# Loading the next group's keys and queries in ten parts of 128 KB, spread over the scores of the current group

## What is computed

```python
x = x + 0.5 * ffn(layernorm(x))
x = x + attention(layernorm(x))       # 16 heads of 16, softmax(q k^T / 4) v, then wo and bo
x = x + 0.5 * ffn(layernorm(x))       # same weights

def ffn(x):                            # k0, k1, k2 are boolean: +1 or -1
    h = relu(s0 * (concat([x, -x]) @ sign(k0))) * 2     # 512 -> 1024
    h = relu(s1 * (h @ sign(k1))) * 2                   # 1024 -> 1024
    return s2 * (h @ sign(k2))                          # 1024 -> 256
```

## Time and profile before

| what | us |
|---|---|
| median of 3 runs (range) | 1506.63 (1505.17 to 1507.43) |
| the profiled execution, its own time | 1504.11 |
| its span, first to last instruction | 1500.2 |
| PE busy / PEld / ACT / DVE / POOL | 1476.9 / 763.4 / 1152.1 / 594.8 / 60.0 |
| mean granted TensorE clock | 0.999 |

### The profile page before, as it was taken

One profiled execution on the slowest core, in us unless ns is written; L12 is line 12 of the kernel. 1 busy time (PEld: TensorE's weight loads), 2 busy tenths in 40 slices (PEclk: granted clock), 3 DMA queues, 4 the chain that ended last, 5 costly groups with the idle time before them and its releaser, 6 DMA issues.

```text
span 1500.2 us, 69702 instructions
## 1 busy us (share of the span) xinstructions
PE 1476.9 (98%) x32431; PEld 763.4 (51%) x32431; DVE 594.8 (40%) x1330; ACT 1152.1 (77%) x1240; POOL 60.0 (4%) x65
## 2 busy tenths in 40 slices
PE   9999999999999999999999999999999999999999
PEld 4555455444455445545454454455455565445454
DVE  7546755612431253334332332342342342333462
ACT  3221221899898999999999998999999999999721
POOL 2010011001000100010100000000000000000000
PEclk9999999999999999999999999999999999999999
DMA  4121324313221331233223123113112212212010
GB/s 139 44 85 43 85 71 113 87 42 98 70 56 47 104 102 58 60 101 100 84 56 89 52 51 103 43 49 106 43 42 70 85 43 70 85 58 54 25 42 17
DMA packets 110285, 103.91 MB, mean 69 GB/s; under 512 B 55846, under 2 KB 95526, under 8 KB 109990
## 3 DMA queue, kind: packets, MB, share of 16 engines
q1 hardware_dynamic: 109158, 98.60, 23.5%
q10 hardware_dynamic: 832, 0.79, 0.2%
HBM read 61.87 MB, written 25.43 MB: 58 GB/s over the span
## 4 chain that ended last, share of the span: by engine, by line
PE 97%; issue 1%; DVE 1%; DMA 1%; ACT 0%; SPq 0%; ACTq 0%
PE psum L870 31%; PE psum L911 30%; PE psum L891 15%; PE psum L764 12%; PE psum L776 3%; PE psum L752 3%; PE psum L783 2%; PE psum L796 1%; DMA den_t<-den_rows 0%; DMA x_sb<-in_x 0%; PE psum L789 0%; ACT prob L966 0%; DVE den_t L1130 0%; DVE xn L996 0%; SPq L1268 0%
## 5 line engine op out<-in xcount | busy, mean ns | idle before, releaser
L966 ACT ACTIVATE prob<-psum 128x1024 f32<-128x1024 f32 x1024 | 1033.7, 1025 | 72.8 <-PE psum L891 33.6
L911 PE MATMUL psum<-prob,v_sb 64*17 64x512 f32 x8192 | 559.6, 589 | 2.5 <-issue 1.8
L891 PE MATMUL psum<-q_st,k_st 64*32 64x512 f16 (+1 forms) x7736 | 500.6, 376 | 2.6 <-issue 2.5
L939 ACT ACTIVATE h_hi<-psum 128x512 f16<-128x512 f32 x183 | 108.3, 597 | 219.0 <-PE psum L764 167.5
L891 PEld LDWEIGHTS psum<-q_st,k_st 64*32 64x32 f16 (+1 forms) x7736 | 162.0, 92 | 196.4 <-ACT prob L966 68.2
L911 PEld LDWEIGHTS psum<-prob,v_sb 64*17 64x17 f32 x8192 | 157.6, 93 | 150.7 <-issue 72.7
L1004 DVE TENSOR_SCALAR h_hi<-psum 128x512 f16<-128x512 f32 x73 | 50.5, 692 | 385.9 <-PE psum L870 385.9
L1006 DVE SCALAR_TENSOR_TENSOR h_lo<-psum,h_hi 128x512 f16<-128x512 f32 x256 | 168.2, 687 | 82.9 <-ACT h_hi L939 80.4
L870 PE MATMUL psum<-h_lo,w 64*32 64x512 f16 (+1 forms) x4688 | 167.7, 376 | 6.1 <-issue 6.1
L870 PE MATMUL psum<-h_hi,w 64*32 64x512 f16 (+1 forms) x4688 | 164.5, 376 | 1.6 <-issue 1.3
L870 PEld LDWEIGHTS psum<-h_hi,w 64*32 64x32 f16 (+1 forms) x4688 | 83.8, 93 | 65.0 <-issue 10.3
(11 more groups left out here) (110 smaller groups left out, 884.1 us busy)
## 6 DMA issues: line engine op xcount, KB each, us to landing
k_st<-k_halves SPq DMA_DIRECT2D x64, 512.0 KB, 4.5
q_halves<-piece SPq DMA_DIRECT2D x32, 256.0 KB, 2.5
q_st<-q_halves SPq DMA_DIRECT2D x64, 128.0 KB, 4.9
x_rows<-x_sb SPq DMA_DIRECT2D x16, 256.0 KB, 2.2
k_halves<-piece SPq DMA_DIRECT2D x16, 256.0 KB, 2.8
att_rows<-o_sb SPq DMA_DIRECT2D x128, 32.0 KB
x_sb<-x_rows SPq DMA_DIRECT2D x8, 512.0 KB, 4.3
att_t<-att_rows SPq DMA_DIRECT2D x16, 256.0 KB
```

The costliest lines, as they stand in the source:

```text
L891: mm = pe.matmul(psum[c, SCORES[(h + r) % len(SCORES)], :], k_st[rows, slot, t * P:(t + 1) * P][:, c], q_st[rows, slot, :], start=True, st ...
L911: mm = pe.matmul(psum[32 * j:32 * j + va, O_BANKS[r], :], v_sb[rows, b * key_tiles + t, GROUP * g4 + j, :], prob[rows, h % PROBS, :], star ...
L939: act.activation(hi, psum[:, bank, :], ACT.Relu).then_inc(act_done, 1)
L966: act.activation(prob[:, to:to + 2, :], psum[:, bank:bank + 2, :], ACT.Exp, scale=score_scale / QK_SCALE ** 2).then_inc(exp_sem, 1)
```

## The change

The four transfers of a group become ten. A `k_st` slot is loaded in four parts of 32 partitions (128 KB each), a `q_st` slot stays one transfer of 128 KB. The parts of group g + 1 are no longer issued together at the first score of group g, but at its turns 0, 2, 5, 7, 10, 12, 15, 17, 20 and 22 (`KEY_TURNS`): `lay_score` lays a step "keys" ahead of those scores, and `sp_keys` waits by `qk_sem` until PE has finished all scores that stand ahead. The count that PE waits for at a group's first score rises from 16 x 4 to 16 x 10. The bytes are the same. PE, ACT, DVE and POOL have the same instructions in the same order; only SP's list is different, by six more transfers in each of the 32 groups.

```diff
--- before.py
+++ after.py
@@ -276,6 +276,9 @@
 
 
 
+    KEY_PARTS = 4
+    GROUP_SCORES = group_steps * STEP_BANKS // 2
+    KEY_TURNS = [5 * k // 2 for k in range(2 * (KEY_PARTS + 1))]
     scores_left = [numbers.held[bank] for bank in SCORES]
 
     def lay_score(no, narrow=False):
@@ -283,6 +286,8 @@
         n, pair = divmod(no, STEP_BANKS // 2)
         if pair == 0:
             work.append(Step("att", n))
+        if no % GROUP_SCORES in KEY_TURNS and no // GROUP_SCORES + 1 < groups:
+            work.append(Step("keys", no // GROUP_SCORES + 1, KEY_TURNS.index(no % GROUP_SCORES)))
         work.append(Step("score", n, pair, narrow=narrow))
 
     def lay_values(tile):
@@ -547,7 +552,7 @@
         FACTOR0, SCALARS = 4, 10
         WEIGHTS_IN = 16 * 10
         LN_STEPS = 2 * tpb + 13
-        STAGE = 16 * 2 * 2
+        STAGE = 16 * 2 * (KEY_PARTS + 1)
         O_MOVE = 16 * 2 * GROUP
 
         x_tiles = x.rearrange("b s d -> (b s) d").rearrange("(t p) d -> p t d", p=P)
@@ -1186,15 +1191,13 @@
         def sp_steps(steps):
             for s in steps:
                 u, m = s.u, s.m
-                if s.kind == "att":
-                    if s.u % group_steps == 0:
-                        g = s.u // group_steps
-                        if g + 1 < groups:
-                            sp_stage(g + 1)
+                if s.kind == "keys":
+                    sp_keys(u, m)
                 elif s.kind == "o":
                     sp_o(u)
                 elif s.kind == "stage":
-                    sp_stage(u)
+                    for part in range(2 * (KEY_PARTS + 1)):
+                        sp_keys(0, part)
                 elif s.kind == "load":
                     sp_load(u)
                 elif s.kind == "flip":
@@ -1237,24 +1240,26 @@
                 sp.wait_ge(x_out[i % RING], stores_until(i))
             load_x(u)
 
-        def sp_stage(g):
-
+        def sp_keys(g, no):
 
             b, g4 = g // (qblocks * block_groups), g % block_groups
             qb = g // block_groups
-            if g % (qblocks * block_groups) == 0:
+            if no == 0 and g % (qblocks * block_groups) == 0:
                 for n in range(2 * kd):
                     sp.wait_ge(piece_out[n], pieces_out(n, qblocks * (b + 1)))
-            if g >= 2:
-                sp.wait_ge(qk_sem, 2 * key_tiles * (g - 1))
+            if g and GROUP_SCORES * (g - 1) + KEY_TURNS[no]:
+                sp.wait_ge(qk_sem, GROUP_SCORES * (g - 1) + KEY_TURNS[no])
             keys = slice(b * seq, (b + 1) * seq)
             queries = slice(qb * BANK, (qb + 1) * BANK)
-            for pair in range(2):
-                slot, h = g % 2 * 2 + pair, GROUP * g4 + 2 * pair
-                dims = slice(h * hd, (h + 2) * hd)
-                k_rows = k_dram[dims, :, keys].rearrange("d c t -> (d c) t")
-                sp.dma_start(k_st[:, slot, :], k_rows.unsqueeze(1).broadcast_to((4 * hd, 2, seq))
-                             ).then_inc(staged[g % 2], 16)
+            pair, part = divmod(no, KEY_PARTS + 1)
+            slot, h = g % 2 * 2 + pair, GROUP * g4 + 2 * pair
+            dims = slice(h * hd, (h + 2) * hd)
+            if part < KEY_PARTS:
+                rows = 4 * hd // KEY_PARTS
+                k_rows = k_dram[dims, :, keys].rearrange("d c t -> (d c) t")[part * rows:(part + 1) * rows, :]
+                sp.dma_start(k_st[2 * rows * part:2 * rows * (part + 1), slot, :],
+                             k_rows.unsqueeze(1).broadcast_to((rows, 2, seq))).then_inc(staged[g % 2], 16)
+            else:
                 sp.dma_start(q_st[:, slot, :], q_dram[dims, :, :, queries].rearrange("d k c t -> (d k c) t")
                              ).then_inc(staged[g % 2], 16)
```

## The result

The changed kernel takes **1489.18 us** (median of 4 runs, 1485.83 to 1493.06) against 1507.03 for the kernel before in the same comparison (4 runs, 1505.17 to 1509.23): a ratio of 0.9875, 95% interval 0.9847 to 0.9903, or 17.9 us. The profiled execution took 1485.83 us, the fastest of the four; its span is 1481.8 us, 18.4 less than before.

A forecast was written before the change was run, and what follows sets the result against it. PE bounds the kernel, its 16 KB instruction loads waiting behind key bursts. 11 us gained, all other terms 0: profiled 1504.1 to 1493.1 us, median 1495.6; range 1490.3 to 1502.0, chance of forecast 0.70.

The forecast's parts named there:

- Nothing changes: Rival: PE's issue waits have another cause that merely falls near a group's start; time stays 1506.6 us; chance 0.09.
- Slower, the last parts come late: Rival: SP issues turn 22's part over 5.9 us late, PE waits at the next group's first score; 1512 us; chance 0.07.
- Half of it comes back: Rival: instruction loads still meet parts, stores and worse-placed 1.5 MB bursts; 1500 to 1501 us; chance 0.14.
- the burst goes: Term for attention: splitting each group's key and query burst ends PE's stalls behind it; 11 us gained.
- fifteen windows: Windows of 9 us behind fifteen key loads in the attention where PE was idle, 9.7 us in all.
- Other bursts stay: Term for the 1.5 MB row fetches: uncut but moved behind key parts; taken as 0, between 4.1 less and 5.2 more.
- Costs at nothing: Terms for SP's queue, waits, last part and group 0, each forecast to cost 0.
- SP's six more issues: Term for SP's queue: 3.6 us more per group, covered by 15 us of waiting at L1256; cost 0.
- the new waits: Term for SP waiting on `qk` at each part's turn, delaying steps behind; cost 0, up to 1 us for DVE.
- the last part: Term for the part issued after turn 22, needed at turn 32: 10.8 us against 4.9 us landing; cost 0.
- group 0's ten issues: Term for issues ahead of the attention, covered by PE's layers; cost 0.
- the case that I followed: Fetch of `den_t`, issued at 929.40, read at 962.60; moved some 14 us later it leaves 19 us for landing.

The follow-up runs named there:

- six_at_once: Changed kernel with each key slot in two parts of 256 KB, six transfers a group, all issued at turn 0: 1503.8 us, ratio 0.9993 to the kernel before.
- ten_at_once: Changed kernel with all ten parts of a group issued at its turn 0: 1485.8 us, ratio 0.9870 to the kernel before.
- fetch_spread: Changed kernel with the 1.5 MB fetches also cut into twelve 128 KB transfers, one issued per turn: 1480.1 us, ratio 0.9830 to the kernel before.
- cut_all: Kernel before with keys in ten parts at turn 0 and fetches in twelve 128 KB transfers issued at once: 1480.5 us, ratio 0.9842.
- four_spread: Changed kernel with whole slots, four transfers of 512 or 128 KB at turns 0, 7, 12 and 20: 1492.7 us, ratio 0.9912 to the kernel before.

## Why the prediction was right, and where it failed

**The cause was right.** Bursts hold up PE's instruction loads; the missing packet of the earlier trace rows and its coming at the burst's end pointed to it. "Nothing changes" fell with the result; the round-robin of the Trainium skill ("DMA: Bandwidth & Descriptors", section Queues, rings and completion order) doesn't describe these instruction loads as they were measured, since an engine's queues taken in turn should have made six_at_once (1503.8 us) and ten_at_once (1485.8) alike; nor was the fetch hidden, as the skill's page "Runtime: NRT & Kernel Launch", section Instruction fetch mechanics, has it. "Slower, the last parts come late" fell too: PE has no wait on a key part. "Half of it comes back" was wrong in its time but right in one thing, the fetches at worse moments, as the second term below shows.

**The step that failed is the term "the burst goes".** I put it at 11 us between 9.7 (PE's idle time in fifteen windows) and 14.3 (by ACT's), and took the lower since it "measures PE directly". Turn by turn it is 16.4 us in those same fifteen windows, and 21.0 us with what followed in the same groups. PE's idle time is no measure of its lost time: the stall of group 6 shows 0.24 us of idle and costs 1.27; over all fifteen, with the second window of groups 3 and 18, 11.1 us of idle stand against 21.0. A likely reason, not tested, is that matmuls overlap and their ends are modelled, so that a stall is partly covered by the records of those before it. ACT's missing busy time, the bound that I passed over, was nearer: 14.3 against 16.4. It saw the turns that didn't happen.

**"Other bursts stay", taken at 0, was -4.1 us** where it isn't bound up with the stalled keys; with the second windows of groups 3 and 18 (+3.7), which I had counted here, it is near 0. I had given it -5.2 to +4.1. The fetches moved behind key parts and met PE at worse moments four times (-1.1 to -2.4 us each). fetch_spread and cut_all show that fetches do cost that much and more, by taking it all away: 9 us against the changed kernel (5 to 7 by the ratios), 5 to 6 against ten_at_once (4 to 6 by the ratios). In the sum the two errors partly cancel: 21.0 - 4.1 = 16.9 instead of 11. That the time came out as close to the range as it did owes something to this luck.

**Costs at nothing held.** Apart from what the fetches' new places cost, no wait of PE comes from SP's six more issues, the new waits or the last part; group 0's ten issues can be behind 0.2 us at most, which PE has lost when the attention begins. The denominators of the case that I followed were issued at 928.48 and first read at 947.25, 19 us later, and weren't late.

**The reason given for the gain was wrong in one word.** I wrote that the burst's ten pieces help because they stand two or three turns apart. ten_at_once shows that they help without standing apart, and six_at_once speaks for the reason: SP can't issue 128 KB transfers as fast as the engines drain them. The forecast number didn't depend on it, but the advice would have.

**My range** stopped at 1490.3 since it took 14.3 as the most that key loads could cost. A bound from the same two rows with its error unknown should have been wider.

**What stays open:** how instruction loads and data share an engine, and why the slack is what it is. Pacing by SP is read from the DMA engines' shares (63% against 99%) and from four_spread; it wasn't varied by itself. Neither a pause between transfers of 256 KB nor 128 KB parts issued faster, from two queues for instance, was tried.

## What to carry to other kernels

A kernel that, like this one with 32431 matmuls in 1500 us, is bound by a long stream of small TensorE instructions can also hang on its instruction loads, and "issue" in PE's waits is the place to see it. If those waits stand some microseconds behind bursts of transfers, cut the transfers until the issuing queue is slower than the engines: here 128 KB, one per 0.6 us, no planning needed. cut_all needs no list of turns and is 9 us faster than the change studied (5 by the ratios).

To price such a stall, align the same instructions of two traces, or count the turns that a steadily working engine missed; PE's idle time gave little more than half.

## What the runs showed that I had not expected

- A useless copy of 1 MB per group that no engine's work waits for cost 16.8 us over 32 groups (21 by the ratios); cut into 128 KB pieces, 2.2 us (4).
- Halving a transfer from 512 to 256 KB in one go won nothing (ratio 0.9993), quartering it won 21 us against the kernel before (ratio 0.9870).
- An issue of keys took SP about the same 0.5 to 0.6 us for 512, 256 and 128 KB.
- The kernels with bursts scatter more: 1496.9 to 1510.7 us for six_at_once in ten runs and 1500.2 to 1510.8 for the kernel before in nineteen, against 1480.1 to 1482.8 for cut_all in four. That would fit stalls which depend on how bursts and instruction loads happen to meet, but wasn't tested by itself.
